# First attention of an audio tower: heads of both batches per step in halves of the array, row sums from ones columns, division after the values

## The chip, the cores and the metric

One program on one NeuronCore of a Trainium2 chip (trn2). The engines are TensorE (PE; PEld is its weight load), VectorE (DVE), ScalarE (ACT), GpSimd (POOL) and SyncE (SP, which issues DMAs here). They run side by side and wait for each other by semaphores. The metric is the device time of one execution in microseconds.

## The reference, cut to what matters

The input is 8 batches of 375 rows of 64 features. The token mixer takes the magnitudes of a real Fourier transform along the rows, which gives S = 189 tokens of 64 features for each batch, and runs this attention over them with 8 heads of width 8. The change is in this one, the first attention:

```python
def _mha(x, in_w, in_b, out_w, out_b):
    qkv = x @ in_w.T + in_b
    q, k, v = jnp.split(qkv, 3, axis=-1)          # 8 heads, dh = 8
    att = softmax(einsum('bhqd,bhkd->bhqk', q, k) / sqrt(dh), axis=-1)
    o = einsum('bhqk,bhkd->bhqd', att, v)
    return o @ out_w.T + out_b
...
a = _mha(src, l_in_w, l_in_b, l_out_w, l_out_b)
src = _layer_norm(src + a, ln1_g, ln1_b)
ff = relu(src @ ff_w1.T + ff_b1) @ ff_w2.T + ff_b2
```

After it come a second attention of one query, a weighted window sum, a retention layer and, for the longest part of the time, an attention over a product-key table. None of these is changed, but for the order of the feed-forward layer's first eight matmuls.

## The kernel before, in words

Batches go in pairs: batch 2p takes partitions 0 to 63 and batch 2p+1 takes 64 to 127, so that NPAIR = 4 pairs fill the 128 partitions. The queries of a pair are cut in two (QT: 95 and 94 rows). A pair takes 8 steps t. In a step one batch `b2` = (t//2)%2 and one group of four heads `hf` = t%2 are worked on, for the query part `qt` = t//4. The four engines each have their order written out, and the steps overlap:

- TensorE, `scores` (L259): four matmuls of 189 columns. The weights are `qz`, the queries of both batches with all features zeroed but those of one head of one batch (`mask_queries`, L490, on VectorE, over 8 heads at a time), so all 128 rows of the array are used for 8 that are not zero. The results go to two PSUM banks.
- VectorE, `row_max` (L481): negated maximum of each row over the four heads (L484), and its product with the scale (L488).
- ScalarE, `exponentials` (L397): four activations (L400), each followed by a read of the accumulated row sum `Z`.
- VectorE takes the reciprocal of the four sums (L512), and GpSimd multiplies the four heads' probabilities with it (L214).
- TensorE, `turn_probabilities` (L267): eight transposes (L274) to PSUM banks 4 and 5. VectorE copies bank 4 to `PT` (L507), ScalarE bank 5 (L411).
- TensorE, `values` (L278): eight matmuls of 95 columns (L287) with 64 columns of weights, `vz`, in which each head's values have their own place and the rest is zero. They add up in bank 6 + qt, at the partitions of batch `b2`; the eight matmuls of a step have the same `b2`.
- ScalarE copies the output of a query part to `oT` (L416), with the value bias `bv1` added.

In TensorE's loop (L299 to L318) step t issues the scores of step t+2, the transposes of t-1 and the values of t-2; the two last value steps of a pair stand behind its loop. ScalarE's and VectorE's loops (L419, L509) follow the same steps. GpSimd also copies the next pair's keys and values (`feed_keys`, `feed_values`).

Every fp32 matmul stands in the trace as two records (x8 for four matmuls); a transpose is one record. Behind the loop come the projection (L323), a layer norm, the feed-forward layer's first eight matmuls (L331: the weights have 64 rows, at the rows of batch `b2`, and `b2` is the outermost loop), eight ReLUs on ScalarE (L433) and its second matmuls (L337: 64 columns of output at the partitions of `b2`). The order on each engine is the program's; no scheduler moves anything. `AHEAD` lists semaphores that start above zero.

## Time and profile before

| | us |
|---|---|
| median of 3 runs | 2034.01 (2032.58 to 2034.33) |
| the profiled execution | 2033.69 |
| its span | 2031.9 |
| loop of the first attention, from the first scores in it to the projection | 42.00 to 160.63 |
| TensorE busy over the span | 1927.7 (95%) |
| VectorE, ScalarE, GpSimd busy over the span | 1638.6, 1475.7, 1340.6 |

The span is what the profile covers; 1.8 us lie around it. The first attention is some 6% of the span, near its start. The 40 slices of the page are 51 us each; this attention is in slices 1 to 4. A number before a row's name in the timeline is its start, the second its length, both in us; a row of several instructions (x8) runs from the first's start to the last's end, and "idle before" is how long the engine stood still. In the grouped view the numbers behind the bar are the busy time in us and the mean of one in ns, then the idle time and what ended it.

### The profile page before, as it was taken

What the parts mean: (1) busy time and instruction counts of PE and PEld (TensorE: products, weight loads), DVE (VectorE), ACT (ScalarE), POOL (GpSimd) and SP (SyncE); (2) the same over time, 40 slices, a digit from 0 to 9 for tenths busy, and PEclk for the clock granted to TensorE, in tenths of its full rate; (3) what the DMA queues carried; (4) which work ended last, traced back from release to release, by engine and by line L of the source; (5) the groups of instructions that cost most, each with busy time, mean ns of one, the idle gap of its engine ahead of it and who ended that gap; (6) DMA issues with size and microseconds to landing.
All of it is one profiled execution on the core that took longest, in us unless ns stands there. A gap on an engine that the chain in (4) does not pass through costs nothing.

```text
span 2031.9 us, 43914 instructions
## 1 busy us (share of the span) xinstructions
PE 1927.7 (95%) x11396; PEld 1514.1 (75%) x11396; DVE 1638.6 (81%) x4903; ACT 1475.7 (73%) x3083; POOL 1340.6 (66%) x1560
## 2 busy tenths in 40 slices
PE   5996749999999999999999999999999999999997
PEld 3984437777777777777777777777777777777776
DVE  3563658888888888888888888888888888888886
ACT  3663237777877777877787777777777777777775
POOL 2440117777777777777777777777777777777775
PEclk9998869999999999999999999999999999999999
DMA  3000030000100020001000100001000100010001
GB/s 99 1 0 0 0 105 21 18 17 17 58 20 19 19 62 20 19 17 59 19 17 19 62 20 19 19 19 62 17 17 17 59 20 19 19 62 20 18 17 28
DMA packets 118154, 58.06 MB, mean 29 GB/s; under 512 B 109712, under 2 KB 116048, under 8 KB 116813
## 3 DMA queue, kind: packets, MB, share of 16 engines
q1 hardware_dynamic: 115298, 56.75, 10.3%
q10 hardware_dynamic: 2795, 0.70, 0.2%
q14 instruction: 48, 0.39, 0.1%
q8 instruction: 13, 0.21, 0.0%
HBM read 24.55 MB, written 0.70 MB: 12 GB/s over the span
## 4 chain that ended last, share of the span: by engine, by line
PE 81%; issue 3%; POOL 1%; DVE 1%; ACT 0%; DMA 0%; SPq 0%; DVEq 0%; POOLq 0%; ACTq 0%
PE ps L989 28%; PE ps L997 15%; PE ps L980 14%; PE ps L1001 8%; PE ps L1039 4%; PE ps L1057 3%; PE ps L974 2%; PE ps L1049 2%; PE ps L1024 2%; PE ps L1011 1%; PE ps L1017 1%; POOL k_W_low L1334 1%; PE ps L1040 0%; SPq L932 0%; DVE k_W L1448 0%
## 5 line engine op out<-in xcount | busy, mean ns | idle before, releaser
L1448 DVE SCALAR_TENSOR_TENSOR k_W<-ps,k_W 128x688 f32<-128x688 f32 x1028 | 892.3, 868 | 236.1 <-ACT k_W L1160 208.8
L1334 POOL TENSOR_TENSOR k_W_low<-k_W,k_W_high 128x688 fp32r<-128x688 f32 x513 | 851.3, 1660 | 334.7 <-ACT k_W_high L1165 334.7
L1160 ACT ACTIVATE k_W<-ps 128x688 f32<-128x688 f32 x1029 | 765.6, 744 | 376.4 <-PE ps L980 358.9
L989 PE MATMUL ps<-k_W,k_tab 128*128 128x344 f32 x2048 | 676.6, 453 | 0.0
L980 PE MATMUL ps<-k_X,k_sel 128*128 128x344 f16 x2058 | 472.6, 311 | 24.9 <-DMA k_X<-k_spl 13.7
L989 PEld LDWEIGHTS ps<-k_W,k_tab 128*128 128x128 f32 x2048 | 366.4, 190 | 127.3 <-issue 0.5
L1165 ACT ACTIVATE k_W_high<-k_W 128x688 fp32r<-128x688 f32 x513 | 395.6, 771 | 0.0
L997 PE MATMUL ps<-k_W_high,k_tab_high 128*128 128x344 f32 x1024 | 386.0, 379 | 0.0
L997 PE MATMUL ps<-k_W_high,k_tab_low 128*128 128x344 f32 x1024 | 325.0, 320 | 0.0
L980 PEld LDWEIGHTS ps<-k_X,k_sel 128*128 128x128 f16 x2058 | 176.4, 99 | 195.9 <-issue 91.5
L1001 PE MATMUL ps<-k_W_low,k_tab_high 128*128 128x344 f32 x1024 | 244.3, 320 | 0.0
L997 PEld LDWEIGHTS ps<-k_W_high,k_tab_high 128*128 128x128 f32 x1024 | 193.6, 189 | 24.7
L997 PEld LDWEIGHTS ps<-k_W_high,k_tab_low 128*128 128x128 f32 x1024 | 193.7, 189 | 0.0
L1001 PEld LDWEIGHTS ps<-k_W_low,k_tab_high 128*128 128x128 f32 x1024 | 177.1, 188 | 0.0
L1328 POOL TENSOR_TENSOR k_spl<-k_aS,k_spl 128x480 f16<-128x480 f32 x65 | 71.8, 1104 | 71.3 <-ACT k_spl L1155 71.3
L1039 PE MATMUL ps<-k_kv,k_qT 128*128 128x128 f32 (+2 forms) x390 | 105.4, 388 | 3.4 <-issue 0.5
L1508 DVE TENSOR_SCALAR k_rc<-k_cand,k_small 128x100 f32<-128x100 f32 x195 | 102.7, 578 | 0.0
L1290 POOL TENSOR_TENSOR k_cand<-k_top 128x192 f32<-128x192 f32 (+1 forms) x132 | 55.1, 437 | 61.6 <-DVE k_top L1404 61.6
L214 POOL TENSOR_TENSOR P<-P,rz 95x756 f32<-95x756 f32 (+1 forms) x32 | 46.2, 1442 | 66.0 <-DVE rz L512 66.0
L1189 ACT ACTIVATE k_P<-ps,k_nmax 128x128 f32<-128x128 f32 (+2 forms) x195 | 86.6, 459 | 2.9 <-DVE k_nmax L1466 2.9
L1057 PEld LDWEIGHTS ps<-k_vw,k_PT 128*128 128x128 f32 (+2 forms) x780 | 83.0, 176 | 0.9 <-ACT k_PT L1195 0.9
L1057 PE MATMUL ps<-k_vw,k_PT 128*128 128x64 f32 (+2 forms) x780 | 82.1, 256 | 0.7 <-ACT k_PT L1195 0.7
(223 smaller groups left out, 2503.2 us busy)
## 6 DMA issues: line engine op xcount, KB each, us to landing
k_tab<-in_tables SPq DMA_DIRECT2D x9, 2048.0 KB, 7.2
k_X<-k_spl SPq DMA_TRANSPOSE x390, 2.4
k_xs<-x2T SPq DMA_DIRECT2D x33, 172.0 KB, 2.1
k_qT<-k_qs SPq DMA_DIRECT2D x33, 86.0 KB, 2.0
cst<-in_consts SPq DMA_DIRECT2D x1, 1024.0 KB, 19.3
wts<-in_weights SPq DMA_DIRECT2D x1, 896.0 KB, 13.4
cst<-in_consts SPq DMA_DIRECT2D x1, 874.5 KB, 17.1
xr<-in_xrows SPq DMA_DIRECT2D x1, 750.0 KB
```

The costliest lines, as they stand in the source:

```text
L980: mm = mm_(ps[:, 2 * (d % 2) + k, 0:LOUT], sel[:, (c // 8) % 2, c % 8, :], X[:, par, c // 8, 0:LOUT], start=True, stop=True)
L989: mm = mm_(sums, tab[:, slot, at + k, :], W[:, d % RING, k, :], start=(d == 0 and k == 0), stop=(d == NDC - 1 and k == 1))
L997: mm_(sums, t[:, slot, at + k, :], W_high[:, q % SPLIT_RING, k, :], start=(d == 0 and k == 0 and t is tab_high), stop=False)
L1001: mm = mm_(sums, tab_high[:, slot, at + k, :], W_low[:, q % SPLIT_RING, k, :], start=False, stop=(d == NDC - 1 and k == 1))
L1039: mm_(ps[0:m, bank, c0:c0 + keys], qT[:, pj, t0:t0 + m], kv[:, 0:keys], start=True, stop=False)
L1057: mm = mm_(ps[0:m, MID1, 64 * t:64 * t + 64], PT[0:kn, kt, t0 - k0:t0 - k0 + m], vw[0:kn, kt, :], start=(kt == 0), stop=(kt == t))
L1160: A(W[:, d % RING, :, :], ps[:, 2 * (d % 2):2 * (d % 2) + 2, 0:LOUT], ACT.Exp).then_inc(e_done, 1)
L1165: A(W_high[:, split_at(d) % SPLIT_RING, :, :], W[:, d % RING, :, :], ACT.Copy).then_inc(high_done, 1)
L1189: A(P[0:m, t, 0:TT[t][0] + m], ps[0:m, bank, c0:c0 + TT[t][0] + m], ACT.Exp, bias=nmax[0:m, t:t + 1], accum_out=zz[0:m, t:t + 1]).then_inc ...
L1334: G.tensor_tensor(W_low[:, q % SPLIT_RING, :, :], W[:, d % RING, :, :], W_high[:, q % SPLIT_RING, :, :].bitcast(F32), ALU.subtract).then_i ...
L1448: V.scalar_tensor_tensor(W[:, d % RING, :, :], ps[:, 2 * (d % 2):2 * (d % 2) + 2, 0:LOUT], 0.0, W[:, d % RING, :, :], ALU.is_ge, ALU.mult) ...
L1508: o = V.tensor_scalar(rc[:, t, :], cand[:, t, :], small[:, MX, t:t + 1], None, ALU.is_ge)
```

## The change

A step now takes head j = t%4 of both groups of four heads and of both batches: four heads, as before, but two of each batch.

- `scores`: the weights of a matmul are the 64 rows of one batch (`rows`), and so are the keys; successive matmuls alternate between rows 0 to 63 and rows 64 to 127, and write to different banks. `qz` has one mask for both batches (`heads`, the sum of the two, with the scale in it), so a pair's masks are two operations of 128 x 756 in place of two of 128 x 1512.
- `values`: successive matmuls alternate between the output partitions of the two batches. Beside the 8 values of a head `vz` has 8 columns of ones, written once by GpSimd, 32 columns away; so the same matmuls give the sums of the exponentials, in eight rows for each head, 32 partitions from the values. The banks are 6 + hf, and both query parts use the same two.
- The read of the row sum, the product with the scale (L488), the reciprocals of the sums (L512), GpSimd's products (L214) and ScalarE's output copies (L416) go. In their place VectorE divides: `divide_by_sums`, eight operations for each query part (four reciprocals of 32 x 95 out of PSUM, four products), before the row maximum of step 5 and behind step 7.
- The value bias goes through the projection once (`bo`, one matmul and one addition in front of the loop).
- TensorE's step t now issues the transposes of t and the values of t-1; one value step stands behind the loop. `P` has two buffers in place of four.
- The feed-forward layer's first matmuls have `b2` innermost, and its ReLUs follow that order.

```diff
-        qz = sb("qz", [128, 2, 2, H, S])
+        qz = sb("qz", [128, 2, H, S])
         kp = sb("kp", [128, 2, S])
-        vz = sb("vz", [95, 2, 2, H * (128 + DH)])
+        vz = sb("vz", [95, 2, 2, 2, 2, 4 * (64 + DH)])
         negmax = sb("negmax", [95, 2, 4])
-        ebias = sb("ebias", [95, 2, 4])
-        P = sb("P", [95, 4, 4, S])
-        Z = sb("Z", [95, 4, 4])
-        rz = sb("rz", [95, 4, 4])
+        bo = sb("bo", [128, 1])
+        heads = sb("heads", [128, H])
+        P = sb("P", [95, 2, 4, S])
+        rz = sb("rz", [128, 95])
         PT = sb("PT", [95, 2, 2, 4 * 95])
         oT = sb("oT", [128, NPAIR, S])
...
-        AHEAD = {pt0_ready: 1, pt1_ready: 1, pv_done: 1, oT_ready: 2}
+        AHEAD = {pt0_ready: 1, pt1_ready: 1, pv_done: 1, oT_ready: 1}
...
+                def head_blocks(rows, par, kt, hf):
+                    return vz[0:rows, par, kt, :, hf, :].rearrange("p b (j x) -> p b j x", j=4)
+
+                pool.wait_ge(vz_zeroed, 1)
+                for par in range(2):
+                    for kt in range(2):
+                        for hf in range(2):
+                            c0 = 32 - 32 * hf
+                            nc.gpsimd.memset(head_blocks(95, par, kt, hf)[:, :, :, c0:c0 + DH], 1.0).then_inc(vz_zeroed, 1)
...
+                        v = vt[0:kn, kt, 128 * p:128 * p + 128] if isinstance(p, int) else vt[0:kn, kt, bass.ds(p * 128, 128)]
+                        for hf in range(2):
+                            c0 = 32 * hf
+                            nc.gpsimd.tensor_copy(head_blocks(kn, par, kt, hf)[:, :, :, c0:c0 + DH],
+                                                  v.rearrange("p (b f j d) -> p b f j d", b=2, f=2, j=4)[:, :, hf]).then_inc(vz_ready, 1)
...
-                        for t in range(8):
-                            n = QT[t // 4][1]
-                            pool.wait_ge(rz_ready, 8 * p + t + 1)
-                            nc.gpsimd.tensor_tensor(P[0:n, t % 4, :, :], P[0:n, t % 4, :, :],
-                                                    rz[0:n, t % 4, :, None].to_broadcast([n, 4, S]), ALU.mult).then_inc(pn_ready, 1)
-                            if t == 2:
...
+                nc.tensor.matmul(ps[:, 3, 400:401], weight("o1"), bias("bv1"), start=True, stop=True).then_inc(bo_mm, 1)
...
                 def scores(par, t):
-                    qt, b2, hf = t // 4, (t // 2) % 2, t % 2
+                    qt, j = t // 4, t % 4
                     q0, n = QT[qt]
-                    for j in range(4):
-                        mm = nc.tensor.matmul(ps[0:n, 2 * hf + j // 2, (j % 2) * S:(j % 2 + 1) * S],
-                                              qz[:, par, b2, 4 * hf + j, q0:q0 + n], kp[:, par, :], start=True, stop=True)
+                    for hf in range(2):
+                        for b2 in range(2):
+                            rows = slice(64 * b2, 64 * b2 + 64)
+                            mm = nc.tensor.matmul(ps[0:n, 2 * (t % 2) + b2, hf * S:(hf + 1) * S],
+                                                  qz[rows, par, 4 * hf + j, q0:q0 + n], kp[rows, par, :], start=True, stop=True)
                     mm.then_inc(score_done, 1)
...
                 def turn_probabilities(k, t):
-                    hf, n = t % 2, QT[t // 4][1]
-                    pe.wait_ge(pn_ready, k + 1)
+                    n = QT[t // 4][1]
                     pe.wait_ge(pt0_ready, k + 1)
                     pe.wait_ge(pt1_ready, k + 1)
...
+                    for kt, (k0, kn) in enumerate(QT):
+                        for g in range(4):
+                            mm = nc.tensor.transpose(ps[0:kn, 4 + kt, 95 * g:95 * g + n],
+                                                     P[0:n, t % 2, g, k0:k0 + kn], const("eye")[0:n, 0:n])
...
                 def values(k, par, t):
 
-                    qt, b2, hf = t // 4, (t // 2) % 2, t % 2
+                    qt, j = t // 4, t % 4
                     n = QT[qt][1]
                     pe.wait_ge(pt0_ready, k + 2)
                     pe.wait_ge(pt1_ready, k + 2)
-                    for j in range(4):
-                        for kt, (k0, kn) in enumerate(QT):
-                            at = 128 * (4 * hf + j) + 64 * b2
-                            mm = nc.tensor.matmul(ps[64 * b2:64 * b2 + 64, 6 + qt, 0:n], vz[0:kn, par, kt, at:at + 64],
-                                                  PT[0:kn, hf, kt, 95 * j:95 * j + n],
-                                                  start=(hf == 0 and j == 0 and kt == 0), stop=(hf == 1 and j == 3 and kt == 1))
+                    for kt, (k0, kn) in enumerate(QT):
+                        for hf in range(2):
+                            for b2 in range(2):
+                                g = 2 * b2 + hf
+                                mm = nc.tensor.matmul(ps[64 * b2:64 * b2 + 64, 6 + hf, 0:n], vz[0:kn, par, kt, b2, hf, 64 * j:64 * j + 64],
+                                                      PT[0:kn, t % 2, kt, 95 * g:95 * g + n],
+                                                      start=(j == 0 and kt == 0), stop=(j == 3 and kt == 1))
                     mm.then_inc(pv_done, 1)
...
-                            if t >= 1:
-                                turn_probabilities(8 * p + (t - 1), t - 1)
+                            turn_probabilities(8 * p + t, t)
                             if t == 1:
                                 pe.wait_ge(vz_ready, 4 * p + 4)
-                            if t >= 2:
-                                if t in (2, 6):
+                            if t >= 1:
+                                if t in (1, 5):
                                     pe.wait_ge(oT_ready, 2 * p + (t // 4 + 1))
-                                values(8 * p + (t - 2), par, t - 2)
-                        turn_probabilities(8 * p + 7, 7)
-                        values(8 * p + 6, par, 6)
+                                values(8 * p + (t - 1), par, t - 1)
                         values(8 * p + 7, par, 7)
...
-                for b2 in range(2):
-                    for hf in range(2):
-                        for g in range(2):
+                for hf in range(2):
+                    for g in range(2):
+                        for b2 in range(2):
                             if b2 == 0 and hf == 0:
                                 pe.wait_ge(ln_done, g + 1)
                             bank = (4 * b2 + 2 * hf + g + 4) % 8
...
+                    n = QT[t // 4][1]
+                    for b2 in range(2):
+                        for hf in range(2):
+                            g = 2 * b2 + hf
+                            a = nc.scalar.activation(P[0:n, t % 2, g, :], ps[0:n, 2 * (t % 2) + b2, hf * S:(hf + 1) * S],
+                                                     ACT.Exp, bias=negmax[0:n, t % 2, g:g + 1])
...
-                    def copy_output(qt):
-                        q0, m = QT[qt]
-                        act.wait_ge(pv_done, 8 * p + (4 * qt + 4) + 1)
-                        nc.scalar.activation(oT[:, bass.ds(p, 1), q0:q0 + m].rearrange("p a s -> p (a s)"),
-                                             ps[:, 6 + qt, 0:m], ACT.Identity, bias=bias("bv1")).then_inc(oT_ready, 1)
...
-                        if t == 6:
-                            copy_output(0)
-                    copy_turned(7)
-                    copy_output(1)
...
+                dve.wait_ge(bo_mm, 1)
+                V.tensor_scalar(bo[:, :], ps[:, 3, 400:401], bias("bo1"), None, ALU.add).then_inc(bo_ready, 1)
...
-                    dve.wait_ge(max_done, k + 1)
-                    V.tensor_scalar(ebias[0:n, hf, :], negmax[0:n, hf, :], DH ** -0.5, None, ALU.mult).then_inc(ebias_done, 1)
-
...
+                    V.tensor_tensor(qz[:, par, 4 * hf:4 * hf + 4, :], q.to_broadcast([128, 4, S]),
+                                    heads[:, 4 * hf:4 * hf + 4, None].to_broadcast([128, 4, S]), ALU.mult).then_inc(qz_ready, 1)
+
+                def divide_by_sums(p, qt):
+                    q0, m = QT[qt]
+                    o = oT[:, bass.ds(p, 1), q0:q0 + m].rearrange("p a s -> p (a s)")
+                    dve.wait_ge(pv_done, 8 * p + (4 * qt + 4) + 1)
+                    for g in range(4):
+                        hf, at, sums = g % 2, 32 * g, 32 * (g + 1 - 2 * (g % 2))
+                        a = V.reciprocal(rz[at:at + 32, 0:m], ps[sums:sums + 32, 6 + hf, 0:m])
+                    a.then_inc(rz_ready, 1)
+                    dve.wait_ge(rz_ready, 2 * p + (qt + 1))
+                    for g in range(4):
+                        hf, at = g % 2, 32 * g
+                        a = V.tensor_tensor(o[at:at + 32], ps[at:at + 32, 6 + hf, 0:m], rz[at:at + 32, 0:m], ALU.mult)
+                    a.then_inc(oT_ready, 1)
...
                         for t in range(8):
-                            n = QT[t // 4][1]
-                            dve.wait_ge(exp_done, 8 * p + t + 1)
-                            V.reciprocal(rz[0:n, t % 4, :], Z[0:n, t % 4, :]).then_inc(rz_ready, 1)
+                            if t == 5:
+                                divide_by_sums(p, 0)
                             row_max(8 * p + (t + 2), (t + 2) % 8)
-                            if t >= 1:
-                                copy_turned(t - 1)
+                            copy_turned(t)
                             if t in (1, 3):
                                 mask_queries(1 - par, (p + 1) % NPAIR, t // 2)
-                        copy_turned(7)
+                        divide_by_sums(p, 1)
```

Of TensorE's order, before, step 3 of a pair: `kp,qz` are the scores, `cst,P` the transposes, `PT,vz` the values.

```order
L300 REGISTER_ALU
L263 MATMUL ps<-kp,qz 94x189 [waits exp_done]
L263 MATMUL ps<-kp,qz 94x189 x3
L274 MATMUL ps<-cst,P 95x95 [waits pt1_ready,pt0_ready,pn_ready]
L274 MATMUL ps<-cst,P 94x95
L287 MATMUL ps<-PT,vz 64x95 [waits pt1_ready,pt0_ready]
L287 MATMUL ps<-PT,vz 64x95 x7
```

And of the change, step 5 of a pair, the first that uses the value banks again:

```order
L305 REGISTER_ALU
L268 MATMUL ps<-kp,qz 94x189 [waits exp_done]
L268 MATMUL ps<-kp,qz 94x189 x3
L278 MATMUL ps<-cst,P 95x94 [waits pt1_ready,pt0_ready]
L278 MATMUL ps<-cst,P 95x94 x3
L278 MATMUL ps<-cst,P 94x94 x4
L318 REGISTER_ALU
L292 MATMUL ps<-PT,vz 64x94 [waits pt1_ready,pt0_ready,oT_ready]
L292 MATMUL ps<-PT,vz 64x94 x7
```

The counts are the same. The transposes no longer wait for GpSimd (`pn_ready`), and are those of the step's own number; the values of step 5 wait for the division of the first query part (`oT_ready`).

Of VectorE's order, before, steps 4 and 5 of a pair: `rz<-Z` is the reciprocal of the sums, `negmax` the row maximum, `PT` the copy of the turned probabilities.

```order
L512 RECIPROCAL rz<-Z 94x4 [waits exp_done]
L483 REGISTER_ALU
L484 TENSOR_REDUCE negmax<-ps 94x4 [waits score_done]
L488 TENSOR_SCALAR ebias<-negmax 94x4 [waits max_done]
L507 COPY PT<-ps 95x380 [waits ptr_done]
```

And of the change, in step 5:

```order
L494 RECIPROCAL rz<-ps 32x95 [waits pv_done]
L494 RECIPROCAL rz<-ps 32x95 x3
L496 ISA
L499 ISA [waits rz_ready]
L499 TENSOR_TENSOR oT<-ps,rz 32x95
L477 REGISTER_ALU
L478 TENSOR_REDUCE negmax<-ps 94x4 [waits score_done]
L517 COPY PT<-ps 95x380 [waits ptr_done]
```

Two small operations a step are gone; the division (its product stands four times) is ahead of the row maximum and of the copy that TensorE's next transposes wait for. Behind step 7 it stands ahead of the next pair's row maximum in the same way.

## Rows read from the trace of the kernel before

**Rows 1.** Windows view: busy us (count) per engine, then granted clock, in mid loop.

```profile
70.00:100.00 30.00, 28.98 (x265) 27.09 (x264) 17.60 (x34) 17.76 (x74) 12.90 (x14) 1.00 0.01 1
```

**Rows 2.** Grouped view, 0 to 300 us, lines of the first attention's loop.

```profile
L400 ACT ACTIVATE P<-ps,ebias 95x189 f32<-95x189 f32 (+1 forms) x136 | 54.5, 409 | 16.9 <-DVE ebias L488 16.3
L263 PE MATMUL ps<-kp,qz 128*95 128x189 f32 (+1 forms) x272 | 50.7, 331 | 7.9 <-ACT P L400 5.4 <-DVE qz L493 2.4
L287 PE MATMUL ps<-PT,vz 95*64 95x95 f32 (+3 forms) x512 | 48.1, 247 | 0.0
L214 POOL TENSOR_TENSOR P<-P,rz 95x756 f32<-95x756 f32 (+1 forms) x32 | 46.2, 1442 | 66.0 <-DVE rz L512 66.0
L484 DVE TENSOR_REDUCE negmax<-ps 95x4 f32<-95x756 f32 (+1 forms) x34 | 31.9, 938 | 41.4 <-PE ps L263 41.1
L400 ACT ACTIVATION_READ_ACCUMULATOR P<-ps,ebias 95x1 f32 (+1 forms) x136 | 26.7, 196 | 0.0
L507 DVE COPY PT<-ps 95x380 f32<-95x380 f32 x32 | 17.3, 542 | 5.4 <-PE ps L274 5.4
L493 DVE TENSOR_TENSOR qz<-qT,cst 128x1512 f32<-128x1512 f32 x10 | 17.3, 1734 | 0.0
```

**Rows 3.** Timeline, one step of the loop on TensorE, and ScalarE's copy in it.

```profile
50.06 1.52 PE L263 MATMUL ps<-kp,qz 128*94 128x189 f32 x8
...
51.41 0.83 PE L274 MATMUL ps<-cst,P 95*95 95x95 f32 x8
...
52.17 1.54 PE L287 MATMUL ps<-PT,vz 95*64 95x95 f32 x16
52.28 0.48 ACT L411 ACTIVATE PT<-ps 95x380 f32<-95x380 f32 x1 [0.46 <-PE ps L274]
...
53.64 1.52 PE L263 MATMUL ps<-kp,qz 128*94 128x189 f32 x8
```

**Rows 4.** Timeline, the pair's end and the next pair's start on TensorE.

```profile
76.00 1.52 PE L263 MATMUL ps<-kp,qz 128*94 128x189 f32 x8 [1.02 <-ACT P L400]
...
157.28 2.84 PE L287 MATMUL ps<-PT,vz 95*64 95x94 f32 x32
...
160.63 1.54 PE L323 MATMUL ps<-oT,wts 128*128 128x378 f32 x4 [0.52 <-ACT oT L416]
```

**Rows 5.** Timeline, matmuls in halves of the array, and the ReLUs.

```profile
168.11 6.19 PE L331 MATMUL ps<-x,wts 64*128 64x378 f32 x16 [2.17 <-DVE x L464]
...
172.99 2.44 ACT L433 ACTIVATE hff<-ps,bia 128x378 f32<-128x378 f32 x5 [0.52 <-PE ps L331]
...
175.48 2.81 PE L337 MATMUL ps<-hff,wts 128*64 128x378 f32 x16 [1.18 <-ACT hff L433]
```

**Rows 6.** Grouped view by form, VectorE, operations near those that are new.

```profile
L475 DVE TENSOR_TENSOR src<-src,cst 128x756 f32<-128x756 f32 x1 | 0.9, 945 | 1.8 <-ACT src L388 1.8
...
L544 DVE COPY p2T<-ps 95x128 f32<-95x128 f32 x1 | 0.3, 288 | 0.8 <-PE ps L359 0.8
L583 DVE RECIPROCAL tsum<-tsum 128x4 f32<-128x4 f32 x1 | 0.2, 171 | 0.0
L539 DVE RECIPROCAL z<-z 128x1 f32<-128x1 f32 x1 | 0.2, 166 | 0.6 <-ACT s L444 0.6
```

**Rows 7.** Timeline, the start of the attention up to the loop.

```profile
33.21 1.91 PE L253 MATMUL ps<-wts,src 128*95 128x128 f32 x16
33.94 3.51 DVE L493 TENSOR_TENSOR qz<-qT,cst 128x1512 f32<-128x1512 f32 x2
...
39.08 0.94 DVE L484 TENSOR_REDUCE negmax<-ps 95x4 f32<-95x756 f32 x1 [1.63 <-PE ps L263]
...
42.00 3.10 PE L263 MATMUL ps<-kp,qz 128*95 128x189 f32 x16 [1.68 <-ACT P L400]
```

**Rows 8.** Windows view: PE, PEld, DVE, ACT, POOL busy, then granted clock.

```profile
29.30:32.40 3.10, 3.10 (x6) 1.66 (x5) 0.00 (x0) 1.15 (x2) 0.00 (x0) 0.50 0.00 0
168.00:175.00 7.00, 6.12 (x16) 3.37 (x16) 0.99 (x3) 3.74 (x8) 0.00 (x0) 0.76 0.00 0
242.00:246.00 4.00, 4.00 (x21) 2.67 (x20) 2.41 (x7) 0.00 (x0) 0.00 (x0) 1.00 0.00 0
```

**Rows 9.** Timeline, the projections at the lower clock.

```profile
31.17 2.20 PE L250 MATMUL ps<-src,wts 128*128 128x378 f32 x4
```

More of the change, by code:

```diff
@@ L204, in _ @@
                 pool.wait_ge(v_ready, 1)
-                pool.wait_ge(vz_zeroed, 1)
+                pool.wait_ge(vz_zeroed, 9)
                 feed_values(0, 0)
@@ L210, in _ @@
                         following = (p + 1) % NPAIR
[L211 to L221 removed]
+                        pool.wait_ge(score_done, 8 * p + 1)
+                        feed_keys(1 - par, following)
+                        pool.wait_ge(pv_done, 8 * p + 1)
+                        feed_values(1 - par, following)
             @block.tensor
@@ L283, in values @@
                     pe.wait_ge(pt1_ready, k + 2)
-                    for j in range(4):
-                        for kt, (k0, kn) in enumerate(QT):
-                            at = 128 * (4 * hf + j) + 64 * b2
-                            mm = nc.tensor.matmul(ps[64 * b2:64 * b2 + 64, 6 + qt, 0:n], vz[0:kn, par, kt, at:at + 64],
-                                                  PT[0:kn, hf, kt, 95 * j:95 * j + n],
-                                                  start=(hf == 0 and j == 0 and kt == 0), stop=(hf == 1 and j == 3 and kt == 1))
+                    for kt, (k0, kn) in enumerate(QT):
[5 more added lines that the diff above has]
+                                                      start=(j == 0 and kt == 0), stop=(j == 3 and kt == 1))
                     mm.then_inc(pv_done, 1)
@@ L324, in _ @@
                 layer_norm(0, x1, res_done, 1, 2)
-                for b2 in range(2):
-                    for hf in range(2):
-                        for g in range(2):
+                for hf in range(2):
+                    for g in range(2):
+                        for b2 in range(2):
                             if b2 == 0 and hf == 0:
@@ L397, in exponentials @@
                 def exponentials(t):
-                    hf, n = t % 2, QT[t // 4][1]
-                    for j in range(4):
-                        a = nc.scalar.activation(P[0:n, t % 4, j, :], ps[0:n, 2 * hf + j // 2, (j % 2) * S:(j % 2 + 1) * S],
-                                                 ACT.Exp, bias=ebias[0:n, hf, j:j + 1], scale=DH ** -0.5,
-                                                 accum_out=Z[0:n, t % 4, j:j + 1])
+                    n = QT[t // 4][1]
[4 more added lines that the diff above has]
+                                                     ACT.Exp, bias=negmax[0:n, t % 2, g:g + 1])
                     a.then_inc(exp_done, 1)
                 for t in range(2):
-                    act.wait_ge(ebias_done, t + 1)
+                    act.wait_ge(max_done, t + 1)
                     exponentials(t)
@@ L496, in _ @@
+                V.tensor_tensor(heads[:, :], const("batch_head")[:, 0:H], const("batch_head")[:, H:2 * H], ALU.add).then_inc(heads_step, 1)
+                dve.wait_ge(heads_step, 1)
+                V.tensor_scalar(heads[:, :], heads[:, :], DH ** -0.5, None, ALU.mult).then_inc(heads_step, 1)
+                dve.wait_ge(heads_step, 2)
                 dve.wait_ge(q_ready, 2)
-                for b2 in range(2):
-                    mask_queries(0, 0, b2)
+                for hf in range(2):
+                    mask_queries(0, 0, hf)
```

43 lines of the change are left out of this document (15 added, 28 removed).

## The prediction

> **What bounds the kernel now.** I looked first at where the first attention lies in the time, then at who is busy in it. The windows view in mid loop shows TensorE busy 28.98 of 30 us at granted clock 1.00 (2.4 GHz), VectorE 17.6, ScalarE 17.8, GpSimd 12.9 [rows 1]. So TensorE bounds this loop. The grouped view names its lines: scores and values with long busy times and almost no idle time, while GpSimd sat idle 66 us before its products and VectorE 41 us before its row maxima [rows 2]. Taking work from GpSimd, or the small operations from VectorE, is worth nothing by itself here. The timeline gives the step: scores start at 50.06, transposes at 51.41, values at 52.17, the next scores at 53.64 [rows 3]. That is 1.35 + 0.76 + 1.47 = 3.58 us, and 32 steps make 114.6 us. The loop takes 118.6 us, from 42.00 to the projection at 160.63 [rows 4, 7]. The rest is about 1 us of waiting for the exponentials at a pair's start, three times [rows 4], and the ends.
>
> **TensorE's step.** The number of matmuls and their columns stay. What changes is which of them stand next to each other. A score record (half of an fp32 matmul, 189 columns) follows the last after 0.17 us: eight take 1.52 us, a lone one 0.33 [rows 2, 3]. A value record follows after 0.086 us: (1.54 - 0.25)/15 [rows 2, 3]. Do matmuls in opposite halves of the array run at the same time? The feed-forward layer's second matmuls alternate between the output halves in fours of records: 16 records of 378 columns take 2.81 us [rows 5]. At twice 0.17 us for twice the columns they would need 5.4 us one after the other, so they overlap fully. For row halves there is the other feed-forward row: 16 records of 378 columns in 6.19 us [rows 5], in a stretch whose mean clock was 0.76 [rows 8]. One after the other at that clock they need 5.4/0.76 = 7.1 us, and part of the 6.19 was spent waiting for the layer norm. So they overlap too, though this row is less clean.
>
> With both, scores fall to 8 x 0.17/2 = 0.68 us and values to 16 x 0.086/2 = 0.69; with transposes of 0.76 that is 2.13 us, the lower end. The upper end adds the whole 0.33 us of a lone record at each of the three changes of pattern: 3.1 us. Before, start times exceed the columns' by about 0.1 us a step; I add 0.3, as a third pattern comes in, and take **2.42 us**.
>
> The Trainium skill, "TensorEngine Tiling (Array Packing)", section Tiling Modes, says that changing the tiling mode drains TensorE. It speaks against this change: a step has three modes in place of two, and the transposes sit between. It gives no price; taken at its word it moves the step toward 3.1 us, and the time toward 2017.
>
> **The other engines in a step of 2.42 us.** Count from the start of scores(t+2). They end at 0.87. VectorE's row maximum takes 0.94, to 1.81, its copy of the turned probabilities 0.54, to 2.39 [rows 2]. The transposes start at 0.8 and end at 1.63, ScalarE copies in 0.48, to 2.11 [rows 3]. Then come the exponentials, at most 4 x 0.41 = 1.64 [rows 2], to 3.8; the reads of the sums are gone. TensorE needs them two steps on, at 4.84, and needs the copies at 3.2. ScalarE's load is 2.12 a step, VectorE's 1.48. The query mask is half as large, 0.945 us by the row of the same shape [rows 6] in place of 1.73 [rows 2]; it lies behind the copy in steps 1 and 3 and ends at 3.35, when the next scores are just ready (3.29). All this is hidden behind TensorE. GpSimd's products, 1.44 us each [rows 2], go and nothing waited long for them: they cost and gain nothing, only the pipeline is a step shorter.
>
> **The division.** Eight VectorE operations on 32 x 94 or 95 elements. No row shows them. The nearest is a copy of 95 x 128 out of PSUM, 0.288 us [rows 6]; the smallest VectorE operations take 0.166. Operations one behind the other start a little before the last one's end, so eight cost between 1.2 and 2.3 us; I take 1.65, nearer the copy's row. VectorE's load for a pair is then 8 x 1.48 + 2 x 0.945 + 2 x 1.65 = 17.0 us against TensorE's 8 x 2.42 = 19.4. But the division is on the path at three places, since both query parts use the same banks:
> - Step 5: TensorE's values of step 5 want it. It starts when the values of step 3 are done, at 0.05, ends at 1.7; TensorE would start at 1.56. Wait 0.2 us, 4 times.
> - Behind step 7: it is queued ahead of the row maximum and of the copy that the next pair's second transposes wait for. Division to 1.7, maximum to 2.66, copy to 3.24. The pair's first step has no values, so TensorE is there at 0.8 + 0.76 + 0.8 = 2.36. Wait 0.9 us, 3 times.
> - At the end nothing covers it: 0.1 + 1.65 + 0.05 = 1.8 us from the last values to the projection.
>
> The loop: 32 x 2.42 = 77.4, + 0.8 + 2.7, + 1.8 = 82.7 us against 118.6: **-35.9**. Its ends: steps of 2.13 and a division of 1.2 give about 70; steps of 3.1 and 2.3 give 109.
>
> **In front of the loop.** VectorE now waits for the extra matmul behind the value projection, which ends at 35.12 [rows 7]. With matmul, addition and two small operations for `heads`, some 0.95 us, the masks start at 36.1 in place of 33.94 and take 1.9 in place of 3.51 [rows 7]: they end at 38.0, not 37.45. Scores in halves give the first row maximum at 38.9 (39.08 before [rows 7]), and without the product and the sum reads the loop starts at about 41.4 in place of 42.00: **-0.6** (between +0.5 and -1). The ones are written while GpSimd waits for the keys.
>
> **Feed-forward.** Before, the first matmuls start at 168.11, the second at 175.48 [rows 5]. The ReLUs run 0.47 us apart when nothing holds them: five in 2.44 [rows 5]. In the new order both batches' matmuls end together. At the lower clock a record takes 0.55 to 0.63 us (four in 2.20 [rows 9], clock 0.50 [rows 8]), so the three later pairs of matmuls end by 169.1 + 3 x 1.26 + 0.15 = 173.1, and two ReLUs later it is 174.0 in place of 175.4: **-1.4** (between 0 and -2.5).
>
> **The sum.** -35.9 - 0.6 - 1.4 = -37.9. Against the profiled execution, 2033.69 (span 2031.9 and 1.8 around it): 1995.8. That execution stands 0.3 below the median of the runs, 2034.01, which changes nothing. The stages behind only start earlier.
>
> **Rivals.**
> - The handshakes bind. Every copy, maximum and exponential is in a circle with TensorE, and VectorE is loaded to 17.0 of 20 us. If hops or drains add up, the step becomes 2.9 us: 32 x 0.48 = +15, about 2011. For it: 3 us of margin in a pair is little. Against: each single deadline above has 0.8 us or more of room, but for the two stalls I count.
> - The reciprocal is slow. An ordinary element costs (1734 - 945)/756 = 1.04 ns [rows 2, 6]. At eight times that, a reciprocal of 95 takes 0.95 us in place of 0.26, a division 2.8 us more, at eight places of the path: +22, about 2018. Against it: a reciprocal of 4 elements takes 171 ns and one of 1 element 166 [rows 6]; three more elements at eight times 1.04 ns would show as 25. That the operands are small and none is in PSUM leaves it some room. The Trainium skill, "VectorE: DVE Perf Modes", section "First, the fixed hardware budget", says that VectorE's reciprocal is an iterative division with a repeat count of 8. By that rule this rival would hold; the trace so far does not agree with it.
> - The change does not do what it says: halves do not overlap, as a lone pair of alternating matmuls with transposes between. The step stays 3.58, the division is covered but for the last 1.8, the pair's 1 us waits go: about 2031.
> - The other side: **TensorE's clock falls.** It was 0.50 in the projections, 0.76 in the feed-forward layer behind the stop-and-go of the layer norm [rows 8]. The new loop idles at each division. At 1.2 GHz a step is 2 x 2.13 + 0.29 = 4.55 us, the loop 147 us, the time about 2061. It decides from 55% of the steps at the lower clock on (35.9 of 64.7 us). Against it: the retention layer's half-array matmuls held 1.00 [rows 8], and the gaps here are under 1 us.
>
> **How the numbers follow.** Forecast 66% (own range 1989 to 2004), handshakes 14%, reciprocal 8%, no overlap 4%, clock 4%, and 4% for better than 1989, since nothing of the 2.42 need be lost between patterns. The range 1988 to 2012 holds forecast and handshakes and leaves out the rest. A measurement tells about 0.2% (4 us) from no change: faster 0.92, same 0.04 (no overlap), slower 0.04 (the clock).
>
> **What would show it.** Right: scores' eight records in some 0.85 us and values' sixteen in 0.9, at clock 1.00; steps of 2.3 to 2.5 us; a TensorE wait of nearly 1 us in a pair's second step for VectorE's copy; reciprocals of 0.25 us; the projection near 125 us. Wrong: records as far apart as before; reciprocals near 1 us; clock 0.50 in the loop; VectorE or ScalarE without idle time in it.

## The result

| | before | after |
|---|---|---|
| median, us | 2034.15 (runs beside the change) | 2082.73 (2076.07 to 2085.59, 4 runs) |
| span of the profiled execution | 2031.9 | 2083.8 |
| loop of the first attention, first scores in it to projection | 118.6 | 156.2 |

The change makes the kernel slower: ratio 1.0231, 95% interval 1.0207 to 1.0255. The forecast was 1995.8. Medians below are of all runs of a kernel, ratios leave out the slow ones, those over 1.5% above its fastest (three of ten in e9, one of ten in e10).

**The clock.** The windows view of after (columns as in [rows 8]) covers the work in front of the loop, the wait ahead of it, its first 57 us, and the stretch of [rows 1]:

```profile
35.00:41.00 6.00, 3.34 (x34) 2.96 (x32) 3.66 (x7) 1.02 (x1) 2.79 (x8) 1.00 0.00 0
41.00:42.60 1.60, 0.00 (x0) 0.00 (x0) 1.04 (x2) 1.37 (x5) 0.46 (x3) 0.69 0.00 0
42.60:100.00 57.40, 54.84 (x383) 42.51 (x384) 30.07 (x45) 21.86 (x64) 1.10 (x5) 0.50 0.01 1
70.00:100.00 30.00, 28.79 (x207) 22.39 (x204) 15.49 (x23) 10.63 (x31) 1.10 (x5) 0.50 0.01 2
```

TensorE is as busy as before, 28.79 of 30 us against 28.98, but at a granted clock of 0.50 (1.2 GHz) where it had 1.00. It fell in the 1.6 us in which TensorE did nothing just ahead of the loop. Busy time alone would not have shown this. In single microseconds the clock is 0.50 until 157 us, then once 1.00 for some 3 us, and it falls again in the wait of the pair's end:

```profile
155.00:160.00 5.00, 4.42 (x42) 3.22 (x38) 3.47 (x7) 0.79 (x3) 0.76 (x4) 0.74 0.00 0
```

**The step.** TensorE's timeline of after, against [rows 3]:

```profile
54.60 1.58 PE L268 MATMUL ps<-kp,qz 64*94 64x189 f32 x8
56.11 1.59 PE L278 MATMUL ps<-cst,P 95*95 95x95 f32 x8
57.63 1.53 PE L292 MATMUL ps<-PT,vz 95*64 95x95 f32 x16
59.09 1.58 PE L268 MATMUL ps<-kp,qz 64*94 64x189 f32 x8
```

A step takes 4.49 us. Scores and values last as long as before at half the clock, so the halves do overlap; the transposes, which have none, doubled.

**The division.** VectorE's timeline at step 5 of the first pair, and TensorE's value step that waits for it:

```profile
63.69 3.05 DVE L494 RECIPROCAL rz<-ps 32x95 f32<-32x95 f32 x4 [0.93 <-PE ps L292]
66.89 1.05 DVE L499 TENSOR_TENSOR oT<-ps,rz 32x95 f32 x4 [0.16 <-DVE rz L494]
```

```profile
68.00 1.52 PE L292 MATMUL ps<-PT,vz 95*64 95x94 f32 x16 [1.35 <-DVE oT L499]
```

A reciprocal of 95 elements takes 0.76 us, a product 0.26. The division is 4.3 us, not 1.65. TensorE's waits from 42 to 200 us, in total, times and longest:

```profile
PE ps L292 <- DVE oT L499: 5.3, 4, 1.3
PE ps L278 <- DVE PT L517: 5.0, 3, 2.6
PE ps L325 <- DVE oT L499: 4.3, 1, 4.3
PE ps L268 <- ACT P L404: 1.8, 1, 1.8
```

They are 16.4 us in all; the last row, 1.8 us, lies in front of the loop, so 14.6 are in it, where the forecast had 5.3. The clock costs more: 32 steps of 4.49 us are 144 us, against 77.4 forecast. Together they make 158.3, some 2 us more than the loop took, which fits the few us at 1.00 near 157.

**The product-key loop.** The view by source line gives its first and last matmul, before and then after:

```profile
L974 PE MATMUL ps<-k_wf,k_xs x384: 272/274/276, 316.9 to 1999.4; 128*128 x128, 128*88 x64
```

```profile
L983 PE MATMUL ps<-k_wf,k_xs x384: 272/274/276, 356.5 to 2050.1; 128*128 x128, 128*88 x64
```

It took 1682.5 us and takes 1693.6: 11.1 us more in code that the change does not touch. The account of the 51.9 us between the spans: the projection starts 38.2 later (198.84 against 160.63 [rows 4]), the product-key loop 39.6 later, which leaves 1.4 for all between; 11.1 inside it; 1.2 behind it.

### The profile page after: what moved, and what is told of

The parts are those of the page before. It is cut to its first block, busy times and chain, and to the rows that moved or that the text cites. A ratio compares the mean times of both kernels' runs of the same rounds, so it can differ in the third digit from the quotient of the medians.

```text
span 2083.8 us, 43755 instructions
## 1 busy us (share of the span) xinstructions
PE 1961.6 (94%) x11398; PEld 1520.3 (73%) x11398; DVE 1649.9 (79%) x4904; ACT 1459.3 (70%) x2939; POOL 1294.8 (62%) x1536
## 4 chain that ended last, share of the span: by engine, by line
PE 79%; issue 3%; POOL 1%; DVE 1%; ACT 1%; DMA 0%; SPq 0%; POOLq 0%; ACTq 0%; DVEq 0%
PE ps L998 27%; PE ps L1006 15%; PE ps L989 14%; PE ps L1010 7%; PE ps L1048 4%; PE ps L1066 3%; PE ps L983 2%; PE ps L1058 2%; PE ps L1033 2%; PE ps L1026 1%; PE ps L1020 1%; POOL k_W_low L1343 1%; PE ps L1049 0%; ACT k_W_high L1174 0%; DVE k_W L1457 0%
## 5 line engine op out<-in xcount | busy, mean ns | idle before, releaser
L1418 DVE MATCH_REPLACE8 k_rp<-k_top,k_sS 128x64 f32<-128x64 f32 (+1 forms) x396 | 78.3, 207 | 0.0
```

## The experiments

Each kernel was timed beside the kernel before on its chip. "Loop" means the time from the first scores in it to the projection, of the profiled execution.

**e1, no division.** The eight operations of a query part become four copies; the sums are not divided out.

```diff
-                        a = V.reciprocal(rz[at:at + 32, 0:m], ps[sums:sums + 32, 6 + hf, 0:m])
-                        a = V.tensor_tensor(o[at:at + 32], ps[at:at + 32, 6 + hf, 0:m], rz[at:at + 32, 0:m], ALU.mult)
+                        a = V.tensor_copy(o[at:at + 32], ps[at:at + 32, 6 + hf, 0:m])
```

> The change, with the division left out: each half bank is copied to oT by four plain copies, no reciprocals and no products (the output is not divided by its sums). Theory 'mix' (in the new loop too little of TensorE's time is work that holds the clock up, because transposes are now a third of it and matmuls run in halves): the clock stays 0.50, a step stays 4.5 us, and only the stalls at the divisions shrink: 4 x 1.5 + 3 x 2.6 + 3 at the end, about 2066 us. Rival 'gaps' (the waits at the slow division, 1.3 to 2.6 us long, pull the clock down): the clock is 1.00 in the loop, a step about 2.4 us, about 1995 us.

2020.81 us, ratio 0.9919 (0.9891 to 0.9948); loop 98.1. Windows and timeline of e1:

```profile
45.00:75.00 30.00, 30.00 (x214) 23.18 (x214) 13.28 (x21) 12.11 (x36) 0.34 (x1) 0.50 0.00 1
75.00:85.00 10.00, 10.00 (x96) 7.98 (x94) 5.76 (x11) 4.75 (x15) 0.77 (x4) 0.68 0.01 2
85.00:115.00 30.00, 29.76 (x396) 23.84 (x398) 22.78 (x41) 21.18 (x61) 1.46 (x6) 1.00 0.00 1
```

```profile
85.70 0.88 PE L268 MATMUL ps<-kp,qz 64*94 64x189 f32 x8
86.52 0.90 PE L278 MATMUL ps<-cst,P 95*95 95x95 f32 x8
87.35 0.88 PE L292 MATMUL ps<-PT,vz 95*64 95x95 f32 x16
88.16 0.88 PE L268 MATMUL ps<-kp,qz 64*94 64x189 f32 x8
```

Without the division's waits the clock comes back some 40 us into the loop and stays. Neither of the two forecasts for this run, 2066 and 1995 us, was met: it lies between them. At the full clock a step takes 2.46 us, 0.82 + 0.83 + 0.81: the predicted step of 2.42 was right for the clock it assumed.

**e2, warm start.** Eight full 378-column matmuls more, four ahead of the two first score steps and four behind them.

```diff
+                pe.wait_ge(k_ready, 2)
+                fill(4)
                 pe.wait_ge(qz_ready, 2)
                 pe.wait_ge(kp_ready, 1)
                 scores(0, 0)
                 scores(0, 1)
+                fill(4)
```

> The change, with eight extra full-array matmuls of 378 columns (results unused) in the two idle stretches of TensorE in front of the loop, so that it enters the loop at clock 1.00. Theory 'mix': the clock falls to 0.50 within the first pair all the same, about 2083 us. Rival 'start' (the loop is only caught at the low clock because it was entered at it): the clock stays 1.00 for the whole loop, steps of about 2.4 us with the slow divisions between: about 2012 us. 'Gaps': it holds 1.00 up to the first division, at step 5, and falls there.

2075.06 us, ratio 1.0180 (1.0117 to 1.0243); loop 144.1. TensorE's timeline of e2 at the first division:

```profile
54.46 0.88 PE L268 MATMUL ps<-kp,qz 64*94 64x189 f32 x8
55.27 0.90 PE L278 MATMUL ps<-cst,P 94*95 94x94 f32 x8
58.88 0.87 PE L292 MATMUL ps<-PT,vz 95*64 95x94 f32 x16 [2.72 <-DVE oT L506]
59.68 0.94 PE L268 MATMUL ps<-kp,qz 64*95 64x189 f32 x8
60.55 1.57 PE L278 MATMUL ps<-cst,P 94*95 94x94 f32 x8
```

Steps run at 1.00 until the first wait for the division, 2.72 us; a few matmuls behind it the same eight transposes last 1.57 us instead of 0.90. The start is one of two places where the clock is lost, and mending it alone is worth little. The clock was back at 1.00 some 10 us later, near 71 us, and fell again at the next wait of this length; so it went on.

**e3, plain transposes.** The transposes become ordinary fp32 matmuls with the identity (two records each): does the kind of instruction keep the clock down?

```diff
-                            mm = nc.tensor.transpose(ps[0:kn, 4 + kt, 95 * g:95 * g + n],
-                                                     P[0:n, t % 2, g, k0:k0 + kn], const("eye")[0:n, 0:n])
+                            mm = nc.tensor.matmul(ps[0:kn, 4 + kt, 95 * g:95 * g + n],
+                                                  P[0:n, t % 2, g, k0:k0 + kn], const("eye")[0:n, 0:n], start=True, stop=True)
```

> The change, with the transposes done as ordinary fp32 matmuls against the identity (16 records of 95 columns a step in place of 8 transposes). Theory 'mix', in the form that transposes do not hold the clock up: the clock is 1.00 in the loop although the step has more work; a step is 0.8 + 1.4 + 0.9 = 3.1 us, and with the slow divisions about 2035 us. Rivals 'gaps' and 'start': the clock stays 0.50, a step is 1.5 + 3.0 + 1.5 = 6.0 us, about 2130 us.

2103.32 us, ratio 1.0319 (1.0254 to 1.0383); loop 181.6. In e3's windows the clock is 0.50 again from 45 to 75 us, and its mean from 85 to 115 us is 0.66:

```profile
45.00:75.00 30.00, 29.94 (x207) 24.74 (x206) 13.17 (x21) 9.78 (x29) 0.00 (x0) 0.50 0.00 1
85.00:115.00 30.00, 25.85 (x206) 21.80 (x202) 16.37 (x27) 9.11 (x26) 0.58 (x4) 0.66 0.01 1
```

So the transposes' kind isn't the cause, or not alone.

**e4, full scores.** The row halves are undone: `qz` has its masks for each batch again, and a score matmul uses all 128 rows. Values, order and division are those of the change.

```diff
-                            rows = slice(64 * b2, 64 * b2 + 64)
-                                                  qz[rows, par, 4 * hf + j, q0:q0 + n], kp[rows, par, :], start=True, stop=True)
+                                                  qz[:, par, b2, 4 * hf + j, q0:q0 + n], kp[:, par, :], start=True, stop=True)
```

> The change with its row halves undone: scores use all 128 rows again with queries masked for one head of one batch (masks of 128 x 1512), values stay in column halves. 'Mix', in the form that half-array matmuls do not hold the clock: 1.00 in the loop, a step of 1.35 + 0.76 + 0.9 = 3.0 us, about 2032 us. 'Mix' in the form that transposes alone matter: scores are a larger share (2.25 of 3.0 us against 1.7 of 2.4), so it may rise too, or flicker. 'Gaps' and 'start': 0.50, a step of 2.7 + 1.5 + 1.5 = 5.7 us, about 2120 us.

2050.18 us, ratio 1.0068 (1.0034 to 1.0101); loop 124.0. TensorE's waits in its loop are 8.9 + 7.0 + 4.3 + 0.4 us, more than the change's 16.4, and yet this kernel is 32 us faster, between its forecasts of 2032 and 2120. Windows of e4:

```profile
55.00:60.00 5.00, 3.71 (x41) 3.28 (x39) 4.76 (x8) 2.19 (x6) 0.00 (x0) 1.00 0.01 3
60.00:65.00 5.00, 4.04 (x31) 3.72 (x32) 3.03 (x7) 1.33 (x4) 0.34 (x1) 0.72 0.00 0
65.00:70.00 5.00, 4.97 (x67) 4.29 (x65) 2.14 (x4) 3.22 (x10) 0.00 (x0) 0.94 0.01 3
```

The clock falls behind a wait here too, and is back within 3 to 7 us, where e1's half-array loop stayed at 0.50 for 40. It doesn't fall behind each wait: of seven waits of 2.2 to 2.4 us, those that end at 60.97, 75.93, 122.08 and 137.02 us were followed by 0.50, those at 93.90, 107.25 and 155.00 were not. Its start differs as well: longer score matmuls leave a gap of 0.45 us ahead of the loop instead of 1.76, so it begins at 1.00.

**e5, ScalarE's instruction count.** The changed kernel has 44 fewer instructions in ScalarE's program ahead of the product-key block (40 reads of sums, and four for the two output copies of its loop, a wait and an activation each). 44 one-column activations are put in their place, with a small tile for them to write.

```diff
+                for k in range(44):
+                    nc.scalar.activation(pad[:, k:k + 1], epst[:, :], ACT.Copy)
```

> The changed kernel with 44 one-column activations (constant in, own column out) added on ScalarE behind its last work in the token mixer, where the trace after shows it idle from 239.9 to 255.3 us: 44 x 0.21 = 9.2 us there, hidden. They bring ScalarE's code back to the length that it had before, for everything behind them. Theory A (the 11 us by which the untouched product-key loop grew, from 1682.5 to 1693.6 us, come from where ScalarE's code lies in memory as it is fetched beside the loads of the tables): the product-key loop is back at 1682 to 1685 us and the kernel takes 2083 - 11 = 2072. Rival B (the 11 us come from the clock's or the tables' state that the attention leaves behind, or from another engine's code): the loop stays at 1693 and the kernel at 2083. Attention itself stays at 156 us in both.

2067.20 us, ratio 1.0147 (1.0106 to 1.0188). The matmul of above, in e5:

```profile
L986 PE MATMUL ps<-k_wf,k_xs x384: 272/274/275, 354.1 to 2035.8; 128*128 x128, 128*88 x64
```

1681.7 us: the 11 us are gone, although the attention is as slow as before the padding (clock 0.50, loop 156.3). The whole kernel gained 15.5 us, since this execution was also 2.4 us ahead when the product-key loop began. ScalarE's timeline says where the 11 us were. The next table is loaded at three places, near 776, 1206 and 1636 us of after. At the first of them, after, before and e5 in turn, its idle times of 2 us and more:

```profile
774.44 0.74 ACT L1169 ACTIVATE k_W<-ps 128x688 f32<-128x688 f32 x1 [2.60 <-issue]
779.57 1.38 ACT L1169 ACTIVATE k_W<-ps 128x688 f32<-128x688 f32 x2 [3.72 <-issue]
```

```profile
734.84 0.74 ACT L1160 ACTIVATE k_W<-ps 128x688 f32<-128x688 f32 x1 [2.58 <-PE ps L989]
```

```profile
771.60 0.74 ACT L1172 ACTIVATE k_W<-ps 128x688 f32<-128x688 f32 x1 [2.43 <-PE ps L1001]
```

Before and e5 stand still once at each place, after twice; the second waits, 3.72, 3.02 and 3.18 us, are 9.9 of the 11.1 us. In nine kernels without the 44 instructions (after, e1 to e4, e6, e8 to e10) the product-key loop took 1690.9 to 1695.6 us, in the three with them (before, e5, e7) 1681.7 to 1683.1. That these are waits for instructions is argued; what is shown is that 44 more activations ahead of the block remove them. They came with a tile of their own, which was not tried alone.

**e6 to e8, the division spread.** A value bank now holds one query part with both groups of heads in it (columns 0 and 128), so VectorE takes the reciprocals of a part in two operations of 128 x 95, and a part's bank is not wanted again for four steps. Each operation stands behind the copy of a different step. e6 has e2's warm start too, e7 also e5's 44 activations, e8 neither.

```diff
-                                mm = nc.tensor.matmul(ps[64 * b2:64 * b2 + 64, 6 + hf, 0:n], vz[0:kn, par, kt, b2, hf, 64 * j:64 * j + 64],
+                                mm = nc.tensor.matmul(ps[64 * b2:64 * b2 + 64, 6 + qt, 128 * hf:128 * hf + n], vz[0:kn, par, kt, b2, hf, 64 * j:64 * j + 64],
...
+                            if t in (0, 2):
+                                sums_reciprocal(8 * p + 1, 2 * p + 1, t // 2, 1)
+                            if t == 4:
+                                divide(4 * p + 2, (p + (NPAIR - 1)) % NPAIR, 1)
+                            if t in (5, 6):
+                                sums_reciprocal(8 * p + 5, 2 * p + 2, t - 5, 0)
+                            if t == 7:
+                                divide(4 * p + 4, p, 0)
```

> Changed kernel with eight full matmuls ahead of the loop (as in e2) and the division taken apart: the value banks hold one query part each (both head halves in one bank, columns 0 and 128), two reciprocals of 128x95 instead of four of 32x95, each behind the copy of another step (previous pair's second part at steps 0 and 2, first part at steps 5 and 6), products at steps 4 and 7; only the last part stands behind the loop. Theory A (TensorE's own long waits let its clock fall, and short half-array work doesn't bring it back): no wait of TensorE is over 1 us in the loop, the granted clock stays at 1.00, a step takes 2.46 us, the loop 32 x 2.46 + about 4 behind it = 83 us against 156; the kernel 2083 - 73 = 2010. Rival B (half-array work doesn't hold the clock in any case): the clock falls some steps into the loop although nothing waits, steps of 4.5 us, loop near 145, kernel 2072. Rival C (VectorE, now at 2.1 to 2.35 us of work in each step, binds): clock 1.00 but steps of 2.7 to 3.0 us, loop 92 to 100, kernel 2019 to 2027.

> e6 with the 44 short activations of e5 behind ScalarE's last work in the token mixer. Theory A of e5: 11 us less than e6 and a product-key loop of 1682 to 1685 us, so 1999. Rival B: as e6.

> e6 without the eight full matmuls: the spread division alone. TensorE enters the loop at a granted clock of 0.50, as in the changed kernel. Theory A (at half clock, half-array work doesn't raise the clock even without long waits): the loop stays at 0.50 for most of its length, steps of 4.5 us, loop 144 + 6 us, kernel about 2075. Rival B (the division's waits alone kept the clock down; e1 without division was at 1.00 after some 40 us): the clock rises 10 to 45 us into the loop, and the loop takes 85 to 105 us, kernel 2015 to 2030.

| | median us | ratio (95%) | loop | product-key loop |
|---|---|---|---|---|
| e6 | 2009.71 | 0.9884 (0.9831 to 0.9937) | 81.0 | 1693.8 |
| e7 | 1996.04 | 0.9801 (0.9761 to 0.9841) | 80.9 | 1683.1 |
| e8 | 2024.26 | 0.9943 (0.9915 to 0.9972) | 98.7 | 1693.6 |

e6 and e7 came out as the theory A of their forecasts (2010 and 1999 us), e8 as its rival B (2015 to 2030). VectorE's timeline of e7, a step with a reciprocal, and two of its windows:

```profile
68.30 0.73 DVE L503 RECIPROCAL rz<-ps 128x94 f32<-128x94 f32 x1
69.34 0.94 DVE L488 TENSOR_REDUCE negmax<-ps 94x4 f32<-94x756 f32 x1 [0.31 <-PE ps L269]
70.20 0.54 DVE L530 COPY PT<-ps 95x380 f32<-95x380 f32 x1
```

```profile
45.00:50.00 5.00, 5.00 (x67) 4.01 (x67) 4.60 (x8) 4.18 (x13) 0.00 (x0) 1.00 0.01 3
115.00:120.00 5.00, 5.00 (x72) 4.08 (x72) 4.26 (x8) 3.54 (x11) 0.00 (x0) 1.00 0.00 0
```

In e6 and e7 TensorE waits nowhere between the loop's start and its last values (2.7 us stand ahead of the projection), VectorE keeps up at 4.2 to 4.8 of 5 us, and the clock is 1.00 in every window from 45 to 120 us. A reciprocal of 128 x 94 takes 0.73 us, as long as one of 32 x 95: more partitions cost nothing here, and two such operations replace four. e8 enters the loop at 0.50 as the change does; its windows in turn:

```profile
70.00:75.00 5.00, 5.00 (x42) 4.21 (x44) 2.50 (x6) 2.00 (x6) 0.00 (x0) 0.50 0.00 0
75.00:80.00 5.00, 5.00 (x37) 3.71 (x34) 2.19 (x4) 1.25 (x4) 0.76 (x4) 0.58 0.00 0
80.00:85.00 5.00, 5.00 (x68) 4.01 (x67) 4.49 (x7) 3.88 (x12) 0.00 (x0) 1.00 0.01 3
```

TensorE worked without a wait from 40.0 us on and had 0.50 until near 79. Against e6 that is 18 us of loop lost to the start alone.

**e9 and e10, the division near the predicted price.** The reciprocals become copies of the same elements (the output is multiplied by the sums), so a division takes 2.3 us, the upper end of the forecast's 1.2 to 2.3; e10 with the warm start.

```diff
-                        a = V.reciprocal(rz[at:at + 32, 0:m], ps[sums:sums + 32, 6 + hf, 0:m])
+                        a = V.tensor_copy(rz[at:at + 32, 0:m], ps[sums:sums + 32, 6 + hf, 0:m])
```

> The changed kernel with the eight reciprocals of a pair replaced by copies of the same elements (0.26 us each by e1, 1.05 for four), so the products multiply by the sums: the division as the prediction priced it, about 2.2 us against 4.3, with its handshakes and its place kept. Theory A (the reciprocals' length is what keeps the clock down once it is down; without that it comes back as in e1): clock 0.50 until 80 to 110 us, then 1.00 with short falls at most; loop 105 to 125 us, kernel 2083 - 30 to 50 = 2033 to 2053. Rival B (any wait at the division, however short, keeps it down): clock 0.50 to the end, waits 2 us shorter at four pair ends and gone at step 5, loop 156 - 12 = 144, kernel 2071.

> e9 with the eight full matmuls ahead of the loop: both conditions as the prediction had them, division of about 2.2 us and TensorE at full clock at the first step. Theory A (with both, the predicted step is right): clock 1.00 for all or nearly all of the loop, steps of 2.46 us, at most 1 us of waiting at each of three pair ends, loop 83 to 90 us, kernel 2010 to 2018. Rival B (short waits alone drop the clock, and half-array work recovers it slowly): it falls at the first pair end near 63 us, loop 115 to 140 us, kernel 2040 to 2068.

e9: 2053.64 us (2026.93 to 2067.61), ratio 1.0018 (0.9970 to 1.0065), loop 129.1. e10: 2036.44 us (2017.26 to 2058.21), ratio 0.9960 (0.9922 to 0.9998), loop 112.9. Timeline and windows of e10:

```profile
57.40 0.87 PE L292 MATMUL ps<-PT,vz 95*64 95x94 f32 x16 [0.72 <-DVE oT L506]
...
67.69 1.31 PE L278 MATMUL ps<-cst,P 95*95 95x95 f32 x8 [1.33 <-DVE PT L524]
```

```profile
65.00:70.00 5.00, 3.67 (x37) 2.98 (x37) 4.21 (x10) 2.78 (x8) 0.00 (x0) 0.80 0.00 0
70.00:75.00 5.00, 5.00 (x40) 3.77 (x39) 2.05 (x3) 2.22 (x8) 0.00 (x0) 0.50 0.00 0
...
100.00:105.00 5.00, 5.00 (x50) 4.06 (x48) 4.43 (x9) 3.15 (x10) 0.00 (x0) 0.78 0.00 0
```

e9 ends just outside its theory A (2033 to 2053 us, loop 105 to 125), and not as A has it: its clock came back near 82 us and fell again near 106, behind a wait of 1.33 us. From there to its last values, near 169 us, TensorE waited for nothing, and the clock stayed at 0.50 for these 63 us; two of its windows:

```profile
105.00:110.00 5.00, 5.00 (x46) 3.89 (x44) 2.59 (x4) 3.00 (x10) 0.00 (x0) 0.57 0.00 0
160.00:165.00 5.00, 5.00 (x37) 4.00 (x36) 1.90 (x3) 1.70 (x5) 0.00 (x0) 0.50 0.00 0
```

e10 is rival B in its mechanism and nearly in its numbers. The waits are close to the forecast's, 0.7 us at step 5 and 1.3 at the pair's end (0.2 and 0.9), and the first is harmless. At the second the clock falls, and returns only past 102 us; then it falls again behind the next such wait, which ends at 124.33 us. The wide spread of both medians fits that: how long a stretch at half clock lasts differs widely, with nothing waiting 10 us (e2), 34 (e10), 38 (e8) and 63 without a return (e9). So a faster reciprocal alone would not have saved the forecast.

## Why the prediction was wrong

- **The rival that held** was the one given 4%, the clock, together with the one given 8%, the slow reciprocal. The step that failed is "against it: the retention layer's half-array matmuls held 1.00, and the gaps here are under 1 us". The gaps were 1.3 to 2.6 us in the loop and 1.76 ahead of it. That first one was in [rows 7] as 1.68 us; before, the full-array loop behind it ran at 1.00. And the forecast had no step for how the clock comes back. It took what held in the retention layer to hold in this loop, and there the trace of before shows another return than in this loop, in its timeline and its windows:

```profile
236.28 2.66 PE L661 MATMUL ps<-r_qk 64*128 64x344 f32 x12 [2.16 <-DVE r_raw L732]
```

```profile
238.00:240.00 2.00, 2.00 (x6) 1.10 (x6) 1.05 (x4) 0.00 (x0) 0.00 (x0) 0.50 0.00 0
240.00:242.00 2.00, 2.00 (x9) 1.37 (x8) 0.53 (x2) 0.00 (x0) 0.00 (x0) 0.77 0.00 0
```

  The retention layer's half-array matmuls, of 344 columns, start behind a wait of 2.16 us. Under them too the clock falls, and it is back at 1.00 some 3 us later, near 241 us, while they run. The new loop's, of 95 and 189 columns, took 10 to 38 us (e2, e8, e10), and in e9 had not done it after 63. So half-array work alone doesn't make the return slow; with full-array scores the same loop needs 3 to 7 us (e4). The rival priced a loop at 1.2 GHz at 147 us; it took 156, since the slow reciprocal's waits came on top.
- **Division, 1.65 us**: 4.3 measured. The nearest row was a copy. The bound from reciprocals of 1 and 4 elements, 166 and 171 ns, misled: 95 elements cost 0.76 us, 8 ns each. The rule weighed beside the rival (Trainium skill, "VectorE: DVE Perf Modes", section "First, the fixed hardware budget") gives the reciprocal a repeat count of 8. An estimate from it and the 1.04 ns of an ordinary element, 8 x 95 x 1.04 ns = 0.79 us, agrees with the trace after. The operands of 1 and 4 elements did not show this price.
- **Step, 2.42 us**: 2.46 at clock 1.00 (e1, e6). Right: 0.33 us above the bare 2.13, where 0.3 was added. It lies in all three parts (0.82, 0.83 and 0.81 against 0.68, 0.76 and 0.69); no run shows how much of it is the drain that the forecast weighed, but the 3.1 us of its upper end is out.
- **Other engines hidden**: right in e6; VectorE keeps up even with the whole division at 2.46 us steps.
- **In front of the loop, -0.6**: it starts at 42.61 instead of 42.00, +0.6. But the projections, which the change doesn't touch, already started 0.7 us later in that execution (29.63 against 28.90), and in e5, with the same code in front, the loop starts at 41.23. The term is too small for these traces to judge.
- **Feed-forward, -1.4**: 207.60 to 213.57, 5.97 us against 7.37 [rows 5]. Right in size, in part by luck: the same code took 4.9 us where its first matmuls ran at the full clock (e4, e7) and 6.5 at the lower (e1, e6, e8).
- **"The stages behind only start earlier"** failed: they start later, and the product-key loop lost 11.1 us, which 44 activations more on ScalarE gave back (e5). No term or rival had it.
- With both faults mended and the 44 activations added, e7 takes 1996.04 us. Its loop of 80.9 us is near the 82.7 forecast; that the total agrees with 1995.8 is no merit of the forecast for the change as made.

Open: what decides whether the clock falls behind a wait. Waits of 0.7 us were harmless in e9 and e10 and each of 1.3 us was followed by a fall, but three of seven above 2 us in e4 were not, nor were those of 2.43 and 1.68 us before. Open too is what makes the return slow in this loop: short matmuls, row halves, or both with the transposes between. Full-array values with half-array scores, or longer matmuls in halves, were not tried. Which other code lengths bring the 11 us wasn't tried.

## What to carry to other kernels

Where a change makes TensorE's work narrower, price the loop at both clocks and ask of each wait, the first one ahead of the loop included, whether a trace shows the work behind it bringing the clock back: here waits of 1.3 us were followed by 34 us and by 63 us at half clock. Take the price of an operation that may be slow for each element from a row with many elements, use all partitions, which cost nothing more here (0.73 us for 128, 0.76 for 32), and spread it over steps. And compare the untouched stages too: a run with the old instruction count tells whether some us hang on it.

## What the runs showed of the hardware

- Half-array matmuls of fp32 run side by side in opposite rows and in opposite column halves: eight score records in 0.82 us and sixteen value records in 0.81 against 1.35 and 1.47, at clock 1.00.
- The granted clock stayed at 0.50 for 38 us of such work with TensorE busy all the time (e8), for 63 us in e9 and 10 in e2. Where it rose to 1.00 it stayed while nothing waited (e1, e6 to e8). Half-array matmuls of 344 columns had it back in some 3 us (retention layer, before).
- VectorE's reciprocal out of PSUM: 0.76 us for 32 x 95, 0.73 for 128 x 94; the product of 32 x 95 0.26 us.
- 44 ScalarE instructions fewer, far ahead of a loop, made that loop longer: 1693.6 us against 1681.7 (after, e5), 1693.8 against 1683.1 (e6, e7). In nine kernels without them it took 1690.9 to 1695.6.
